# Paged attention in split fp32: the fourth head of each quad joins the split, and two small steps change engine

## The chip, the cores and the metric

One core of a Trainium2 chip runs the whole kernel. The metric is the device time in microseconds of one execution; the median of three runs is given. The engines are TensorE (PE in the profile, its weight loads PEld), VectorE (DVE), ScalarE (ACT), GpSimd (POOL) and SyncE (SP), which issues most of the DMAs.

## What is computed

32 sequences of 32 tokens, width 512. Layer one is attention over a paged cache: 32 query heads and 8 key heads of 128, 16 pages of 32 cached positions and the 32 new positions for each sequence.

```python
q = rope(rmsnorm(x @ Wq.T)); k = rope(rmsnorm(x @ Wk.T)); v = x @ Wv.T
k_all = concat([k_cache[table], k], axis=1)      # 512 cached + 32 new columns
v_all = concat([v_cache[table], v], axis=1)
scores = einsum('bqhd,bkhd->bhqk', q, k_all) * SCALE   # cached columns masked by length
probs = softmax(scores)                          # 4 query heads share a key head
o = einsum('bhqk,bkhd->bqhd', probs, v_all) @ Wo.T
```

A convolution along the sequence, an adapter layer and a gated feed-forward layer follow; the change doesn't touch them.

## The kernel before

The 32 sequences are done in two halves of HB = 16 (`Fori` over h). In a half come the projections with norm and rotation, then attention, then the output projection and the later layers. In attention every engine runs a written-out program of steps. A step is one key head g of one sequence b; 8 steps make a sequence, and `GU = 4` steps a quad. The four query heads that share a key head give 4 x 32 = 128 rows, so a step's scores are 128 rows by `LK` = 544 columns, 512 cached and 32 new.

Each engine works strictly through its own list, and counting semaphores order the engines among each other. For a head g:

- ScalarE (`upper_keys`, L781) rounds the keys of head g + 2 to fp32r, k_hi, when the scores of head g are done, since k_hi has two buffers. GpSimd (`lower_keys`, L605) forms the rest, keys minus k_hi. Queries are split once per quad: ScalarE writes q_hi (`upper_q`, L773) at g % 4 == 0, VectorE q_lo = q - q_hi (`lower_q`, L1512) at g % 4 == 1.
- TensorE (`scores`) adds q_hi k_hi, q_hi k_lo and q_lo k_hi, two matmuls each (288 and 256 columns), L1033 to L1044. That is so for three heads of a quad (`NS` = 3). The fourth head is scored in plain fp32 from q_now, a copy of the queries (L774), and the keys as loaded, L1021 and L1023, with no k_hi and no lowering.
- VectorE (L1553) scales by the row factor, adds the mask and takes the minimum in one pass into one of four probability buffers (`PRING`). ScalarE (L822) takes exp with the row sum, VectorE (L1563) the reciprocal of the sum.
- GpSimd (`scale_probs`) scales the 32 new columns into `prob_new` (L591) and the 512 cached ones in place (L593), two steps behind its lowering.
- TensorE transposes the cached part of head g - 2 (`turn_probs`, L1056) into one PSUM bank. VectorE copies that bank to SBUF (L1559), and TensorE multiplies by the values of head g - 3 (`values`, L1088). The next transposes wait until the copy has read the bank.
- Once per quad TensorE transposes the 128 new columns of four heads (`turn_new`, L1068, at g = 5 and g = 1). ScalarE copies four 32x128 quadrants of the result into the block diagonal of `spread` (`spread_new`, L800, at g % 4 == 1), which was cleared once. TensorE multiplies the new values by it (`values_new`, L1098, at g = 7 and g = 3), and ScalarE moves the finished quad out (`keep_o`, L807, at g % 4 == 0).

ScalarE's step, in its order: k_hi of head g + 2 (not where that is a fourth head), exp of g, at g % 4 == 0 q_hi and q_now and later `keep_o`, at g % 4 == 1 `spread_new`, at g = 3 the mask of the next sequence (L786, L787). VectorE's step: the reduction of g, the copy of transposed probabilities of g - 2, the reciprocal of g, at g % 4 == 1 q_lo. SyncE loads pages of keys and values two sequences ahead.

Of the kernel before, what the change touches and what calls it, by code (L numbers as in the profile page):

```python
# [13 lines left out]
ds = bass.ds  # L14
# [15 lines left out]
NS = GU - 1  # L30
NSB = UNITS * NS
# [29 lines left out]
               ("opr", 4), ("opi", 4), ("omr", 4), ("omi", 4)]  # L61
# [17 lines left out]
def constants():  # L79
# [13 lines left out]
    put("seqpos", (p % SEQ)[:, None])  # L93
    put("lmask", LORA_SCALING * (p[:, None] // RANK == np.arange(GRP * SEQ)[None, :] // SEQ))
# [11 lines left out]
def build(nc, xT_d, w_d, amat_d, bmT_d, kpages_d, vpages_d, lA_d, lB_d, rows_d, vcT_d, bp_d, dls_d,  # L106
# [6 lines left out]
    with ExitStack() as ctx:  # L113
# [24 lines left out]

        q_hi = sb("q_hi", [P, 2, NS * D], F32R)
        q_lo = sb("q_lo", [P, 2, NS * D], F32R)  # L140
        q_now = sb("q_now", [P, 2, D])
# [199 lines left out]
        q_copied = sem("q_copied")  # L341
# [10 lines left out]
        spread_clear = sem("spread_clear")  # L352
# [207 lines left out]
        def _(pool):  # L560
# [10 lines left out]
            with pool.Fori(0, HALVES) as h:  # L571
# [11 lines left out]
                def scale_probs(b, g, early=False):  # L583

                    u, a = g // GU, g % GU
                    pool.wait_ge(rinv_ready, h * STEPS + b * HK + g + 1)
                    if a == 0 and not early:
                        pool.wait_ge(new_turned, h * QUADS + b * UNITS + u - 1)
                    pool.sem_inc(pool_past, 1)
                    main, new = prob(g % PRING)[:, 0:LC], prob(g % PRING)[:, LC:LK]  # L590
                    nc.gpsimd.tensor_scalar(prob_new[:, u, a * SEQ:(a + 1) * SEQ], new, rinv[:, g:g + 1], 1.0,  # L591
                                            ALU.mult, ALU.mult).then_inc(new_scaled, 1)
                    nc.gpsimd.tensor_scalar(main, main, rinv[:, g:g + 1], 1.0, ALU.mult, ALU.mult)\  # L593
                        .then_inc(p_ready, 1)

                def lower_keys(b, par, first, last=False):


                    for g in range(HK):
                        s = h * STEPS + b * HK + g  # L600
                        if g % GU < NS:
                            e = g // GU * NS + g % GU
                            pool.wait_ge(khi_ready, (h * HB + b) * NSB + e + 1)
                            pool.sem_inc(pool_past, 1)
                            nc.gpsimd.tensor_tensor(  # L605
                                kbuf_lo(par)[:, :, g, :], kbuf(par)[:, :, g, :],
                                k_hi[:, e % 2, :].rearrange("p (j t) -> p j t", t=PSIZE), ALU.subtract)\
                                .then_inc(klo_ready, 1)
                        if g >= 2:
                            scale_probs(b, g - 2, first)  # L610
                        elif not first:
                            scale_probs(b - 1, g - 2 + HK)
# [31 lines left out]
        def _(act):  # L644
# [18 lines left out]
            with act.Fori(0, HALVES) as h:  # L663
# [107 lines left out]
                def upper_q(u, at):  # L771

                    nc.scalar.activation(q_hi[:, u, :], qo[:, ds(at, NS * D)], ACT.Copy).then_inc(qhi_ready, 1)  # L773
                    nc.scalar.activation(q_now[:, u, :], qo[:, ds(at + NS * D, D)], ACT.Copy).then_inc(q_copied, 1)  # L774

                def upper_keys(b, par, g):
# [3 lines left out]
                    e = g // GU * NS + g % GU  # L780
                    nc.scalar.activation(k_hi[:, e % 2, :].rearrange("p (j t) -> p j t", t=PSIZE),  # L781
# [8 lines left out]
                def spread_new(b, u):  # L790

                    act.wait_ge(new_turned, h * QUADS + b * UNITS + u + 1)
                    if isinstance(b, int) and b == 0 and u == 0:
                        act.wait_ge(spread_clear, h + 1)
                    else:
                        act.wait_ge(o_done, h * QUADS + b * UNITS + u)
                    act.sem_inc(act_past, 1)
                    for a in range(GU):
                        rows = slice(a * SEQ, (a + 1) * SEQ)
                        nc.scalar.activation(spread[rows, a * P:(a + 1) * P], PS[rows, 2560:2688], ACT.Copy)\  # L800
                            .then_inc(spread_ready, 1)
# [8 lines left out]
                def step(b, par, g, first, last=False):  # L810
                    s = h * STEPS + b * HK + g
                    if (g + 2) % GU < NS and not (last and g + 2 >= HK):
# [15 lines left out]
                    if g % GU == 1 and not (first and g < GU):  # L828
                        spread_new(b if g > GU else b - 1, int(g < GU))
# [34 lines left out]
                spread_new(HB - 1, 1)  # L864
# [53 lines left out]
        def _(pe):  # L918
# [9 lines left out]
            with pe.Fori(0, HALVES) as h:  # L928
# [76 lines left out]
                def scores(b, par, g, first):  # L1005
# [4 lines left out]
                    raw = kbuf(par)  # L1010
# [7 lines left out]
                    if a == NS:  # L1018
                        pe.wait_ge(q_copied, h * (QUADS + 1) + b * UNITS + u + 1)
                        pe.wait_ge(k_in[par], h * (136 * HB) + (b - par) * 136 + 272)  # L1020
                        nc.tensor.matmul(PS[:, at:at + mid], q_now[:, u, :], raw[:, 0:SPLIT, g, :],  # L1021
                                         start=True, stop=True)
                        nc.tensor.matmul(PS[:, at + mid:at + LK], q_now[:, u, :], raw[:, SPLIT:NPP + 1, g, :],  # L1023
                                         start=True, stop=True).then_inc(s_ready, 1)
                        return
                    if a == 0:
                        pe.wait_ge(qlo_ready, h * (QUADS + 1) + b * UNITS + u + 1)
                    e = u * NS + a
                    pe.wait_ge(khi_ready, (h * HB + b) * NSB + e + 1)
                    hi, lo = k_hi[:, e % 2, :], kbuf_lo(par)  # L1030
# [710 lines left out]
```

## Time and profile before

| | |
|---|---|
| median of 3 runs | 1304.55 us (1303.5 to 1306.85) |
| profiled execution | 1306.34 us, its span 1304.4 us |
| TensorE matmuls busy | 1246.8 us, 96% of the span |
| VectorE, ScalarE, GpSimd busy | 812.0, 809.2, 759.2 us |
| mean granted TensorE clock | 0.988 of full speed |
| read from HBM | 203.33 MB |

The profile comes from one execution. A busy time counts every moment in which an instruction of the engine was open; matmuls are pipelined, so their busy time can include waiting that follows on a chain elsewhere. Durations of one instruction include its start-up, and neighbours on an engine overlap a little, so distances from start to start are the safer measure.

### The profile page before, as it was taken

What the parts mean: (1) busy time and instruction counts of PE and PEld (TensorE: products, weight loads), DVE (VectorE), ACT (ScalarE), POOL (GpSimd) and SP (SyncE); (2) the same over time, 40 slices, a digit from 0 to 9 for tenths busy, and PEclk for the clock granted to TensorE, in tenths of its full rate; (3) what the DMA queues carried; (4) which work ended last, traced back from release to release, by engine and by line L of the source; (5) the groups of instructions that cost most, each with busy time, mean ns of one, the idle gap of its engine ahead of it and who ended that gap; (6) DMA issues with size and microseconds to landing.
All of it is one profiled execution on the core that took longest, in us unless ns stands there. A gap on an engine that the chain in (4) does not pass through costs nothing.

```text
span 1304.4 us, 28634 instructions
## 1 busy us (share of the span) xinstructions
PE 1246.8 (96%) x7378; PEld 1040.6 (80%) x7378; DVE 812.0 (62%) x1725; ACT 809.2 (62%) x2258; POOL 759.2 (58%) x885
## 2 busy tenths in 40 slices
PE   7899988999999998998999999889999999999998
PEld 6678877889999895764777788778989999878856
DVE  5976655776767766862328766556767767655422
ACT  5566766788878874332326766667878878743320
POOL 4344457788888874533214434568888888744330
PEclk9999999999999998998999999999999999999999
DMA  7244379999999935304243432798999999433300
GB/s 246 97 130 130 98 198 250 225 237 236 236 227 232 239 78 180 137 1 146 81 142 115 134 124 98 199 247 212 234 243 225 232 233 232 106 110 134 97 33 33
DMA packets 148008, 214.82 MB, mean 165 GB/s; under 512 B 24980, under 2 KB 119510, under 8 KB 142166
## 3 DMA queue, kind: packets, MB, share of 16 engines
q1 hardware_dynamic: 130566, 204.86, 58.6%
q10 hardware_dynamic: 17328, 9.04, 2.4%
q8 instruction: 30, 0.49, 0.2%
q14 instruction: 52, 0.43, 0.1%
q0 software_dynamic: 32, 0.00, 0.0%
HBM read 203.33 MB, written 10.49 MB: 164 GB/s over the span
## 4 chain that ended last, share of the span: by engine, by line
PE 77%; DVE 6%; SPq 5%; issue 4%; DMA 4%; ACT 2%; ACTq 1%; POOL 0%; DVEq 0%; POOLq 0%
PE PS L1088 15%; PE PS L1056 8%; PE PS L956 4%; PE PS L950 4%; PE PS L952 4%; PE PS L1098 4%; PE PS L1153 3%; PE PS L1150 3%; PE PS L1144 3%; PE PS L1195 2%; SPq L475 2%; PE PS L936 2%; SPq L462 2%; PE PS L1021 2%; PE PS L1023 2%
## 5 line engine op out<-in xcount | busy, mean ns | idle before, releaser
L605 POOL TENSOR_TENSOR kv_parts<-kv,k_hi 128x544 fp32r<-128x544 f32 x192 | 258.7, 1348 | 56.8 <-ACT k_hi L781 53.2
L1088 PE MATMUL PS<-probT,kv 128*128 128x128 f32 x2048 | 272.7, 277 | 6.9 <-DMA kv<-in_vpages 6.9
L1088 PEld LDWEIGHTS PS<-probT,kv 128*128 128x128 f32 x2048 | 250.6, 193 | 7.9 <-DMA kv<-in_vpages 6.0
L565 POOL TENSOR_TENSOR ring_parts<-ring,kv_parts 128x512 fp32r<-128x512 f32 x96 | 128.1, 1338 | 217.7 <-ACT kv_parts L671 187.8
L1559 DVE COPY probT<-PS 128x512 f32<-128x512 f32 x256 | 175.5, 686 | 3.1 <-PE PS L1056 3.1
L822 ACT ACTIVATE ring<-ring,smin 128x544 f32<-128x544 f32 x192 | 143.8, 749 | 45.6 <-DVE smin L1553 41.7
L1553 DVE CUSTOM_DVE_ANT_0 ring<-PS,mask,rq 128x544 f32<-128x544 f32 x192 | 149.8, 780 | 22.2 <-PE PS L1044 13.9
L781 ACT ACTIVATE k_hi<-kv 128x544 fp32r<-128x544 f32 x192 | 125.9, 656 | 60.4 <-PE PS L1044 52.3
L627 POOL TENSOR_TENSOR ring_parts<-ring,kv_parts 128x512 fp32r<-128x512 f32 x64 | 89.2, 1398 | 104.2 <-ACT kv_parts L876 104.2
L593 POOL TENSOR_SCALAR ring<-ring,rinv 128x512 f32<-128x512 f32 x192 | 135.3, 704 | 0.0
L1056 PE MATMUL PS<-consts,ring 128*128 128x128 f32 x768 | 117.7, 276 | 6.8 <-DVE probT L1559 5.9
L1589 DVE TENSOR_TENSOR qo_parts<-qo,kv_parts 128x512 fp32r<-128x512 f32 x64 | 83.0, 1322 | 63.4 <-ACT kv_parts L878 62.4
L591 POOL TENSOR_SCALAR ring<-ring,rinv 128x32 f32<-128x32 f32 x192 | 77.0, 401 | 72.9 <-DVE rinv L1563 72.9
L1056 PEld LDWEIGHTS PS<-consts,ring 128*128 128x128 f32 x768 | 88.2, 141 | 28.2 <-issue 19.8
L950 PE MATMUL PS<-kv_parts 128*128 128x512 f32 x352 | 103.4, 414 | 6.0 <-DVE PS L1474 4.7
L1153 PE MATMUL PS<-qo_parts,kv_parts 128*128 128x512 f32 x256 | 104.4, 408 | 4.9 <-DVE qo_parts L1589 4.9
L1144 PE MATMUL PS<-kv_parts 128*128 128x512 f32 x256 | 102.9, 402 | 4.3 <-ACT kv_parts L878 4.3
L876 ACT ACTIVATE kv_parts<-ring 128x512 fp32r<-128x512 f32 x64 | 40.3, 630 | 104.6 <-PE PS L1144 104.4
L1150 PE MATMUL PS<-kv_parts,ring_parts 128*128 128x512 f32 x256 | 102.5, 400 | 0.8 <-POOL ring_parts L627 0.8
L1553 DVE CUSTOM_DVE_ANT_0 prob<-PS,mask,rq 128x544 f32<-128x544 f32 x64 | 50.2, 784 | 82.0 <-PE PS L1044 80.9
L1563 DVE RECIPROCAL rinv<-rsum 128x1 f32<-128x1 f32 x256 | 41.9, 164 | 90.7 <-ACT ring L822 68.7
L1470 DVE TENSOR_TENSOR kv<-PS,kv 128x512 f32<-128x512 f32 x80 | 55.1, 689 | 67.4 <-ACT prob L706 39.6
(223 smaller groups left out, 2855.2 us busy)
## 6 DMA issues: line engine op xcount, KB each, us to landing
kv<-in_kpages SPq DMA_DIRECT2D x512, 128.0 KB, 2.8
kv<-in_vpages SPq DMA_DIRECT2D x512, 128.0 KB
ring<-in_w SPq DMA_DIRECT2D x44, 1024.0 KB, 4.9
v_new<-kv ACTq DMA_DIRECT2D x16, 256.0 KB, 4.8
k_new<-kv ACTq DMA_DIRECT2D x16, 256.0 KB, 2.4
kv<-k_new SPq DMA_DIRECT2D x32, 128.0 KB, 2.6
kv<-v_new SPq DMA_DIRECT2D x32, 128.0 KB
kv<-in_xT SPq DMA_DIRECT2D x8, 256.0 KB, 5.6
```

Of the source, the lines that this page charges most:

```text
L565: nc.gpsimd.tensor_tensor(slot_lo(n % SLOTS)[:, c, :], slot(n % SLOTS)[:, c, :], block_hi[:, (n % 2) * KC + c, :], ALU.subtract)\
L593: nc.gpsimd.tensor_scalar(main, main, rinv[:, g:g + 1], 1.0, ALU.mult, ALU.mult)\
L605: nc.gpsimd.tensor_tensor(kbuf_lo(par)[:, :, g, :], kbuf(par)[:, :, g, :], k_hi[:, e % 2, :].rearrange("p (j t) -> p j t", t=PSIZE), ALU.s ...
L822: nc.scalar.activation(a, a, ACT.Exp, scale=-1.0, bias=smin[:, g:g + 1], accum_out=rsum[:, g:g + 1]).then_inc(exp_done, 1)
L950: nc.tensor.matmul(dst, x_hi[:, c, ms], hi[:, c, :], start=(c == 0), stop=False)
L1056: mm = nc.tensor.transpose(PS[:, 2048 + c * P:2048 + (c + 1) * P], prob(g % PRING)[:, c * P:(c + 1) * P], ident)
L1088: mm = nc.tensor.matmul(PS[:, at:at + D], vbuf(bpar)[:, c, gg * D:(gg + 1) * D], probT[:, g % 2, c * P:(c + 1) * P], start=(c == 0 and a = ...
L1144: mm = nc.tensor.matmul(bank(c), whi[:, a, cs], ohi[:, a, :], start=(head == 0), stop=False)
L1150: nc.tensor.matmul(bank(c), w[:, cs], ohi[:, a, :], start=False, stop=False)
L1153: mm = nc.tensor.matmul(bank(c), whi[:, a, cs], o, start=False, stop=(head == HQ - 1))
L1553: V.tensor_tensor_reduce(prob(g % PRING)[:, 0:LK], PS[:, at:at + LK], mask[:, par, :], rq[:, par, g:g + 1], 3.0e38, ALU.add, ALU.min, smin ...
L1559: V.tensor_copy(probT[:, g % 2, :], bank(4)).then_inc(pt_main, 1)
```

## The change

All four heads of a quad are scored from the split parts. q_hi and q_lo get four heads of columns, q_now and its semaphore go, and k_hi and the lowering are done for every head. The 32 new columns are scaled by ScalarE (`scale_new`, one head behind its exp) instead of GpSimd. The block diagonal is written by VectorE in one product of the transposed columns, broadcast four times, with a constant 128x4 pattern (`quad`, 1 where row / 32 equals the column), broadcast along each block of 128; it stands behind q_lo at g % 4 == 1. ScalarE's four copies and the clearing of `spread` go.

```diff
...
-               ("opr", 4), ("opi", 4), ("omr", 4), ("omi", 4)]
+               ("quad", GU), ("opr", 4), ("opi", 4), ("omr", 4), ("omi", 4)]
...
+    put("quad", p[:, None] // SEQ == np.arange(GU)[None, :])
...
-        q_hi = sb("q_hi", [P, 2, NS * D], F32R)
-        q_lo = sb("q_lo", [P, 2, NS * D], F32R)
-        q_now = sb("q_now", [P, 2, D])
+        q_hi = sb("q_hi", [P, 2, GU * D], F32R)
+        q_lo = sb("q_lo", [P, 2, GU * D], F32R)
...
-    def scale_probs(b, g, early=False):
-        u, a = g // GU, g % GU
+    def scale_probs(b, g):
...
-        if a == 0 and not early:
-            pool.wait_ge(new_turned, h * QUADS + b * UNITS + u - 1)
...
-        main, new = prob(g % PRING)[:, 0:LC], prob(g % PRING)[:, LC:LK]
-        nc.gpsimd.tensor_scalar(prob_new[:, u, a * SEQ:(a + 1) * SEQ], new, rinv[:, g:g + 1], 1.0,
-                                ALU.mult, ALU.mult).then_inc(new_scaled, 1)
+        main = prob(g % PRING)[:, 0:LC]
...
         for g in range(HK):
-            s = h * STEPS + b * HK + g
-            if g % GU < NS:
-                e = g // GU * NS + g % GU
-                pool.wait_ge(khi_ready, (h * HB + b) * NSB + e + 1)
-                pool.sem_inc(pool_past, 1)
-                nc.gpsimd.tensor_tensor(
-                    kbuf_lo(par)[:, :, g, :], kbuf(par)[:, :, g, :],
-                    k_hi[:, e % 2, :].rearrange("p (j t) -> p j t", t=PSIZE), ALU.subtract)\
-                    .then_inc(klo_ready, 1)
+            pool.wait_ge(khi_ready, h * STEPS + b * HK + g + 1)
+            pool.sem_inc(pool_past, 1)
+            nc.gpsimd.tensor_tensor(
+                kbuf_lo(par)[:, :, g, :], kbuf(par)[:, :, g, :],
+                k_hi[:, g % 2, :].rearrange("p (j t) -> p j t", t=PSIZE), ALU.subtract)\
+                .then_inc(klo_ready, 1)
             if g >= 2:
-                scale_probs(b, g - 2, first)
+                scale_probs(b, g - 2)
             elif not first:
                 scale_probs(b - 1, g - 2 + HK)
...
     def upper_q(u, at):
-        nc.scalar.activation(q_hi[:, u, :], qo[:, ds(at, NS * D)], ACT.Copy).then_inc(qhi_ready, 1)
-        nc.scalar.activation(q_now[:, u, :], qo[:, ds(at + NS * D, D)], ACT.Copy).then_inc(q_copied, 1)
+        nc.scalar.activation(q_hi[:, u, :], qo[:, ds(at, GU * D)], ACT.Copy).then_inc(qhi_ready, 1)
     def upper_keys(b, par, g):
...
-        e = g // GU * NS + g % GU
-        nc.scalar.activation(k_hi[:, e % 2, :].rearrange("p (j t) -> p j t", t=PSIZE),
+        nc.scalar.activation(k_hi[:, g % 2, :].rearrange("p (j t) -> p j t", t=PSIZE),
...
-    def spread_new(b, u):
-        act.wait_ge(new_turned, h * QUADS + b * UNITS + u + 1)
-        if isinstance(b, int) and b == 0 and u == 0:
-            act.wait_ge(spread_clear, h + 1)
-        else:
-            act.wait_ge(o_done, h * QUADS + b * UNITS + u)
+    def scale_new(b, g):
+        u, a = g // GU, g % GU
+        act.wait_ge(rinv_ready, h * STEPS + b * HK + g + 1)
+        if a == 0 and not (isinstance(b, int) and b == 0):
+            act.wait_ge(new_turned, h * QUADS + b * UNITS + u - 1)
...
-        for a in range(GU):
-            rows = slice(a * SEQ, (a + 1) * SEQ)
-            nc.scalar.activation(spread[rows, a * P:(a + 1) * P], PS[rows, 2560:2688], ACT.Copy)\
-                .then_inc(spread_ready, 1)
+        nc.scalar.activation(prob_new[:, u, a * SEQ:(a + 1) * SEQ], prob(g % PRING)[:, LC:LK], ACT.Copy,
+                             scale=rinv[:, g:g + 1]).then_inc(new_scaled, 1)
...
-        if (g + 2) % GU < NS and not (last and g + 2 >= HK):
+        if not (last and g + 2 >= HK):
...
             upper_q(u, nb * (HQ * SEQ) + u * GU * D)
-        if g % GU == 1 and not (first and g < GU):
-            spread_new(b if g > GU else b - 1, int(g < GU))
+        if g:
+            scale_new(b, g - 1)
+        elif not first:
+            scale_new(b - 1, HK - 1)
...
-    spread_new(HB - 1, 1)
+    scale_new(HB - 1, HK - 1)
...
-        raw = kbuf(par)
...
-        if a == NS:
-            pe.wait_ge(q_copied, h * (QUADS + 1) + b * UNITS + u + 1)
-            pe.wait_ge(k_in[par], h * (136 * HB) + (b - par) * 136 + 272)
-            nc.tensor.matmul(PS[:, at:at + mid], q_now[:, u, :], raw[:, 0:SPLIT, g, :],
-                             start=True, stop=True)
-            nc.tensor.matmul(PS[:, at + mid:at + LK], q_now[:, u, :], raw[:, SPLIT:NPP + 1, g, :],
-                             start=True, stop=True).then_inc(s_ready, 1)
-            return
         if a == 0:
...
-        e = u * NS + a
-        pe.wait_ge(khi_ready, (h * HB + b) * NSB + e + 1)
-        hi, lo = k_hi[:, e % 2, :], kbuf_lo(par)
+        pe.wait_ge(khi_ready, s + 1)
+        hi, lo = k_hi[:, g % 2, :], kbuf_lo(par)
...
-        pe.wait_ge(klo_ready, (h * HB + b) * NSB + e + 1)
+        pe.wait_ge(klo_ready, s + 1)
...
-            pe.wait_ge(spread_ready, GU * (h * QUADS + b * UNITS + u))
+            pe.wait_ge(spread_ready, h * QUADS + b * UNITS + u)
         nc.tensor.transpose(PS[:, 2560:2688], prob_new[:, u, :], ident).then_inc(new_turned, 1)
...
-            pe.wait_ge(spread_clear, h + 1)
...
-        pe.wait_ge(spread_ready, GU * (h * QUADS + b * UNITS + u + 1))
+        pe.wait_ge(spread_ready, h * QUADS + b * UNITS + u + 1)
...
+    def spread_new(b, u):
+        dve.wait_ge(new_turned, h * QUADS + b * UNITS + u + 1)
+        if not (isinstance(b, int) and b == 0 and u == 0):
+            dve.wait_ge(o_done, h * QUADS + b * UNITS + u)
+        dve.sem_inc(dve_past, 1)
+        V.tensor_tensor(spread.rearrange("p (a x) -> p a x", a=GU),
+                        PS[:, 2560:2688].unsqueeze(1).to_broadcast([P, GU, P]),
+                        con("quad").unsqueeze(2).to_broadcast([P, GU, P]), ALU.mult)\
+            .then_inc(spread_ready, 1)
     def step(b, par, g, first):
...
-                lower_q(u, ds(nb * (HQ * SEQ) + u * GU * D, NS * D))
+                lower_q(u, ds(nb * (HQ * SEQ) + u * GU * D, GU * D))
+                if not (first and g < GU):
+                    spread_new(b if g > GU else b - 1, int(g < GU))
     for g in range(HK):
...
-            V.memset(spread, 0.0).then_inc(spread_clear, 1)
     for g in range(HK):
...
+    spread_new(HB - 1, 1)
...
```

## Rows read from the trace of the kernel before

**Rows 1.** Windows: length, busy us (and count) by engine, granted clock, DMA share, GB/s.
```profile
198.00:202.00 4.00, 1.55 (x13) 1.29 (x12) 1.73 (x5) 2.44 (x7) 4.00 (x6) 1.00 0.97 276
...
260.00:360.00 100.00, 100.00 (x759) 90.49 (x758) 70.45 (x178) 81.54 (x198) 85.16 (x115) 1.00 0.97 237
```

**Rows 2.** Timeline, first reduction of a quad: quads 1, 7 and 32, first half.
```profile
170.34 0.79 DVE L1553 CUSTOM_DVE_ANT_0 prob<-PS,mask,rq 128x544 f32<-128x544 f32 x1 [3.10 <-PE PS L1044]
...
236.79 0.78 DVE L1553 CUSTOM_DVE_ANT_0 prob<-PS,mask,rq 128x544 f32<-128x544 f32 x1 [1.13 <-PE PS L1044]
...
476.95 0.78 DVE L1553 CUSTOM_DVE_ANT_0 prob<-PS,mask,rq 128x544 f32<-128x544 f32 x1 [1.05 <-PE PS L1044]
```

**Rows 3.** Chain of waits in time order: start, us, engine and line.
```profile
367.11 0.49 PE PS L1021 x2
367.60 0.43 PE PS L1023 x2
368.03 0.51 PE PS L1056 x4
...
370.29 0.13 PE PS L1033
...
371.06 0.44 PE PS L1056 x4
```

**Rows 4.** Timeline of one quad, 361.7 to 371.4: start, us, engine, line, idle before.
```profile
361.72 0.78 DVE L1553 CUSTOM_DVE_ANT_0 prob<-PS,mask,rq 128x544 f32<-128x544 f32 x1 [1.07 <-PE PS L1044]
...
362.55 0.75 ACT L822 ACTIVATE prob<-prob,smin 128x544 f32<-128x544 f32 x1 [0.36 <-DVE smin L1553]
...
363.30 0.51 ACT L773 ACTIVATE q_hi<-qo 128x384 fp32r x1
...
364.03 0.60 ACT L807 ACTIVATE qo<-PS 128x512 f32 x1
...
364.63 0.75 ACT L822 ACTIVATE ring<-ring,smin 128x544 f32<-128x544 f32 x1
...
365.51 0.16 DVE L1563 RECIPROCAL rinv<-rsum 128x1 f32<-128x1 f32 x1 [0.30 <-ACT ring L822]
...
365.89 0.57 DVE L1512 TENSOR_TENSOR q_lo<-qo,q_hi 128x384 fp32r<-128x384 f32 x1 [0.22 <-issue]
...
366.38 0.77 DVE L1553 CUSTOM_DVE_ANT_0 ring<-PS,mask,rq 128x544 f32<-128x544 f32 x1
...
366.54 0.66 ACT L781 ACTIVATE k_hi<-kv 128x544 fp32r<-128x544 f32 x1
...
367.08 0.68 DVE L1559 COPY probT<-PS 128x512 f32<-128x512 f32 x1
...
367.38 1.34 POOL L605 TENSOR_TENSOR kv_parts<-kv,k_hi 128x544 fp32r<-128x544 f32 x1 [0.18 <-ACT k_hi L781]
...
367.88 0.42 PEld L1056 LDWEIGHTS PS<-consts,ring 128*128 128x128 f32 x4 [0.26 <-issue]
...
371.35 0.78 DVE L1553 CUSTOM_DVE_ANT_0 prob<-PS,mask,rq 128x544 f32<-128x544 f32 x1 [1.14 <-PE PS L1044]
```

**Rows 5.** Groups by line and shape: count, busy us and mean ns, idle before.
```profile
L1470 DVE TENSOR_TENSOR kv<-PS,kv 128x512 f32<-128x512 f32 x80 | 55.1, 689 | 67.4 <-ACT prob L706 39.6 <-ACT probT L706 27.8
...
L787 ACT ACTIVATE mask<-consts,lens_b 128x512 f32<-128x512 f32 x32 | 22.7, 709 | 0.0
```

**Rows 6.** The same groups between 360 and 372 us.
```profile
L593 POOL TENSOR_SCALAR ring<-ring,rinv 128x512 f32<-128x512 f32 x5 | 3.5, 695 | 0.0
...
L786 ACT ACTIVATE rq<-rowscale 128x8 f32 x1 | 0.2, 192 | 0.0
```

**Rows 7.** Timeline of VectorE and GpSimd, output projection, 563 to 565 us.
```profile
563.23 1.29 POOL L627 TENSOR_TENSOR ring_parts<-ring,kv_parts 128x512 fp32r<-128x512 f32 x1 [1.50 <-ACT kv_parts L876]
...
563.39 1.15 DVE L1398 TENSOR_TENSOR kv<-consts,kv 128x4 f32<-128x4 f32 x1
```

More of the change, by code:

```diff
@@ L29 @@
 UNITS = HK // GU
-NS = GU - 1
-NSB = UNITS * NS
 SLOTS = 4
@@ L340, in build @@
         qhi_ready = sem("qhi_ready")
-        q_copied = sem("q_copied")
         qlo_ready = sem("qlo_ready")
@@ L351, in build @@
         new_turned = sem("new_turned")
-        spread_clear = sem("spread_clear")
         spread_ready = sem("spread_ready")
@@ L1525, in norm_rows @@
                     dve.wait_ge(qhi_ready, h * (QUADS + 1) + 1)
-                    lower_q(0, slice(0, NS * D))
+                    lower_q(0, slice(0, GU * D))
                     dve.wait_ge(row_ready, 16 * (h + 1))
```

## The prediction

> **What bounds the kernel now.** I read the windows first, then TensorE's chain of waits, then the timeline of one group of four heads, because only the last can say what a change in the order of work is worth. The two attention loops are the stage that is edited: 2 halves, each 16 sequences of 8 key heads, so 64 groups of four heads ("quads"). The window shows TensorE busy for all of its 100 us at the granted clock 1.00, with GpSimd busy for 85, ScalarE for 82 and VectorE for 70 [rows 1]. From that alone one would call TensorE the bound and every other engine free. The distance between the first scores of consecutive quads is (476.95 - 236.79) / 25 = 9.61 us in the steady part [rows 2].
>
> The chain of waits shows what TensorE does with it [rows 3]. A head scored in fp32 takes 0.49 + 0.43 = 0.92 us, a head scored from the split parts takes 371.06 - 370.29 = 0.77 us. The four transposes behind the fp32 head take 0.51 us, those behind a split head 0.44. So the fp32 head is 0.15 us dearer, and 0.07 us of something else sits behind it.
>
> The timeline names that something [rows 4]. VectorE's copy of transposed probabilities (L1559) begins at 367.08 and lasts 0.68, thus ends at 367.76. TensorE's next weight load, for the next transposes, begins 0.12 us later at 367.88, with an idle of 0.26 us in front. The PSUM bank that the transposes write has to be copied out first. TensorE therefore waits once per quad on VectorE, briefly, and the busy share (a pipelined matmul counts as busy) hides it. Followed backwards from that copy, with t = 0 at the start of the quad's first reduction (361.72), the chain is: exp of head 4 on ScalarE at 0.83; q_hi at 1.58; keep_o at 2.31; exp of head 5 at 2.91; reciprocal of head 5 on VectorE at 3.79; q_lo at 4.17; the reduction of head 6 (L1553) at 4.66; the copy for head 4 at 5.36, its end at 6.04; and from there 371.35 - 367.76 = 3.59 us of transposes, values, new values and scores until the next quad's first reduction. 6.04 + 3.59 = 9.63 us. (Heads are counted as in the loop, g = 4 to 7 for this quad; g = 0 to 3 goes the same way.) There is no slack in this chain: each step of it starts when the one before ends, apart from hand-over times. Whatever the change puts into it is paid in every quad.
>
> **The change, part by part.**
>
> *TensorE.* The fourth head of each quad goes from 0.92 to 0.77 us and its transposes from 0.51 to 0.44: 0.22 us less, so TensorE alone could do a quad in 9.63 - 0.22 = 9.41 us. This is worth something only if VectorE's copy comes earlier by as much. It does not, as follows.
>
> *ScalarE at g = 4.* q_hi grows from 384 to 512 columns and q_now goes. Together these two took 364.03 - 363.30 = 0.73 us. q_hi of 512 columns should occupy 0.52 (a 128x512 copy lasts 0.60 [rows 4], and neighbours overlap by about 0.09). Behind it now comes scale_new of head 3, 32 columns with a per-partition scale. A 128x8 copy lasts 0.19, and a 128x512 operation with a per-partition bias 0.71 where the plain one lasts 0.60 [rows 4 to 6]: 0.19 + 0.02 + 0.11 less the overlap of 0.09 is 0.22 us. Bounds: nothing, if it slips into the overlap, and 0.32 without any overlap. Sum 0.74 for 0.73: keep_o still starts at 2.31. TensorE's transpose of the new columns waits for that scale_new, which ends at about 1.58 + 0.52 + 0.31 = 2.4, plus 0.1 of hand-over. If TensorE gets there earlier it waits, by an estimate some tenths. It then still reaches the transposes of g = 7, now at 6.16 (367.88), well before the 7.83 worked out below: up to 1.6 us of such a wait would vanish in the longer one.
>
> *ScalarE at g = 5.* Head 7 now is split too, so its k_hi stands before the exp of head 5, which had no such copy in front before. It waits for nothing (the scores of head 5 are long ready): 366.54 to 367.20 in the rows of head 8, +0.66 us. The exp of head 5 moves from 2.91 to 3.57; its mask and minimum are ready by 2.9, so nothing else hides this. Behind it in ScalarE's queue are scale_new of head 4, k_hi of head 8 and the exp of head 6. The four quadrant copies that leave ScalarE stood behind the exp of head 5, off the chain, so their going saves nothing.
>
> *VectorE at g = 5.* The reciprocal moves to 3.57 + 0.88 = 4.45 and q_lo becomes ready at 4.83. But GpSimd, which had no keys to lower here, now runs the lowering of head 7: it starts 0.84 after its k_hi (366.54 to 367.38), at 2.91 + 0.84 = 3.75, and lasts 1.34, to 5.09. A VectorE operation with two SBUF inputs does not run beside a GpSimd one: a product of 128x4 that needs 0.16 or so (as the reciprocal) took 1.15 us and ended at 564.54, when a GpSimd subtraction of 563.23 + 1.29 = 564.52 did [rows 7]. q_lo has two SBUF inputs, so it starts at 5.09: +0.26. Bounds: 0, if it is not held; +0.97, if GpSimd's next operation (the scaling of the probabilities, 0.70 us [rows 6]) is let in first. q_lo itself has 512 columns for 384: 0.49 / 384 x 128 is 0.16, less the fixed part 0.13 us. The new product follows, 128x512 with one PSUM and one SBUF input: the nearest row lasts 0.69 [rows 5] while GpSimd was working, so it is not held; neighbours overlap by 0.07, +0.62 us. Both its waits (the transposed columns, the last use of the buffer) are met by then. Its bounds are 0.62 and, if both broadcasts and a fresh fetch cost, 0.95. Queued behind it are the reduction of head 6 and the copy that TensorE waits for.
>
> *Sum for a quad.* 0.01 + 0.66 + 0.26 + 0.13 + 0.62 = 1.68, say 1.67 us: the copy ends at 7.71 instead of 6.04, and the transposes' load starts at 7.83. What follows the copy (3.59 us) contains no fp32 work and stays; its lower bound, should those transposes run without their present hitch, is 3.5. New period 11.3 us for 9.63.
>
> *What else fits.* GpSimd: four lowerings of 1.34 and four scalings of 0.70 are 8.2 us of 11.3; the small scalings that leave it had cover. ScalarE some 8 us. Neither decides. The keys of head 7 are lowered by 5.1, before TensorE, held by the transposes, can use all of them. The wider constants, the removed memset and the end of each half cost nothing: they lie beside TensorE's work, and the last spread takes 0.7 us on VectorE where ScalarE's four copies took more.
>
> *How many quads.* From the seventh quad on, 26 per half (25 intervals and the last quad's own), 52 in all: 52 x 1.67 = 87 us. The first six of a half take 236.79 - 170.34 = 66.5 us in the first half, 8.8 above the steady pace, and similar in the second, because pages are late. A slower quad hides those waits: 6 x 11.3 = 67.8, that is 1.3 us more than now if all overlaps and 10 if nothing does. I take 3 per half, 6. Together +93 us. The profiled execution lasted 1306.34 us with a span of 1304.4, 1.8 above the median of 1304.55; 1306.3 + 93 = 1399.3, and on the median's footing 1397.5 us.
>
> *A rule on the lock.* The Trainium skill, "SBUF — State Buffer", section "SBUF: two separate sides", says that the port pair shared by VectorE and GpSimd is an exclusive lock which whichever starts first keeps for the whole instruction. Rows 7 agree. By the rule q_lo must wait for the lowering, as summed; without it the sum would be 52 x 0.26 = 14 us less. The page does not say who comes first at the hand-over, so it also carries rival B.
>
> **The rivals.**
>
> A (forecast, 0.64): the chain as above, 1397.5 us. On its own, with the small bounds, 1380 to 1412.
>
> B (0.12): at 5.09 GpSimd's scaling takes the ports ahead of the waiting q_lo. Another 0.70 per quad, 52 x 0.70 = 36: 1434 us. For it: GpSimd's next operation is ready. Against: VectorE has been waiting longer.
>
> C (0.13): the exp of head 5 does not move, since what precedes it slips elsewhere, or q_lo is not held and the overlaps are kinder: 1.67 - 0.66 = 1.01 per quad, 52 x 1.01 + 6 = 59: 1363 us. Against: in the rows ScalarE goes from keep_o to that exp with no gap.
>
> D (0.06, other side): TensorE sets the pace and the insertions are absorbed; 9.41 for 9.63 gives 52 x 0.22 = 11 us less, 1293 us. It decides only if the copy has 1.7 us of slack before TensorE needs it. The rows show 0.12 us, the hand-over itself. For it speaks only the busy share.
>
> E (0.03): TensorE, now idle 1.6 to 1.9 us per quad, is granted the lower of its two clock levels (1.2 for 2.4 GHz) in places and its instructions in the chain take twice as long there; the stretch behind the copy, 3.59 us, is mostly its own, and over half the quads that is 26 x 3.59 = 93 more, 1490 us. Against: a stretch in which it was busy for 1.55 of 4 us had 1.00 granted all the same [rows 1].
>
> F (0.02): gain and cost cancel, 1304 us.
>
> **From this to the numbers.** A change within 0.3% (4 us) cannot be told from none here. Faster 0.06 (D), same 0.02 (F), slower 0.92 (A, B, C, E). The range runs from C's side, 1358, to B's, 1438; outside lie D, E, F and the ends of B and C.
>
> **What the new profile would show.** Quads 11.3 us apart; TensorE's busy share in the steady windows near 0.85, its main wait at the transposes of L1056 at g = 7 and 3, released by VectorE's copy; a k_hi between keep_o and the exp of head 5; q_lo longer than 0.7 us by its hold; the product at 0.69. The forecast is wrong if VectorE or ScalarE idle between those pieces, if the product costs much more than 0.69, or if quads come at 9.4.

## The result and the profile after

The changed kernel takes 1375.66 us (median of 4 runs, 1374.76 to 1377.74) against 1305.7 us for the kernel before in the same runs: a ratio of 1.0539, 95% interval 1.0515 to 1.0562, 70 us slower. The forecast was 1397.5 us in a range of 1358 to 1438. The profiled execution lasted 1377.74 us with a span of 1375.9, 71.5 us above the span before.

The busy times of the engines over the whole span, and the steady window that answers to [rows 1]:

```profile
PE 1251.8 (91%) x7506; PEld 1047.2 (76%) x7506; DVE 873.8 (64%) x1787; ACT 812.8 (59%) x2256; POOL 781.0 (57%) x693
```

```profile
260.00:360.00 100.00, 88.98 (x686) 80.62 (x685) 69.27 (x163) 71.72 (x176) 77.64 (x74) 1.00 0.82 204
```

TensorE is still the busiest engine. In the steady part all of them are less busy than before, TensorE at 89% for 100, VectorE at 69, ScalarE at 72, GpSimd at 78, and the granted clock is still 1.00. Every engine waits more, and no other engine has filled up: in a window, a chain across engines looks like this. The reductions that open a quad, quads 1, 7 and 32 of the first half (timeline, for [rows 2]):

```profile
169.96 0.78 DVE L1538 CUSTOM_DVE_ANT_0 prob<-PS,mask,rq 128x544 f32<-128x544 f32 x1 [2.97 <-PE PS L1019]
...
239.64 0.78 DVE L1538 CUSTOM_DVE_ANT_0 prob<-PS,mask,rq 128x544 f32<-128x544 f32 x1 [1.11 <-PE PS L1019]
...
513.50 0.78 DVE L1538 CUSTOM_DVE_ANT_0 prob<-PS,mask,rq 128x544 f32<-128x544 f32 x1 [1.07 <-PE PS L1019]
```

(513.50 - 239.64) / 25 = 10.95 us for 9.61 before. The first six quads take 69.7 us for 66.5.

One quad in the timeline answers to [rows 4]. L805 is the exp, L761 q_hi, L783 scale_new, L790 keep_o, L767 k_hi, L1548 the reciprocal, L1486 q_lo, L1520 the product, L1538 the reduction, L1544 the copy, L593 GpSimd's lowering, L584 its scaling and L1031 the transposes:

```profile
371.09 0.79 DVE L1538 CUSTOM_DVE_ANT_0 prob<-PS,mask,rq 128x544 f32<-128x544 f32 x1 [1.12 <-PE PS L1019]
...
371.92 0.75 ACT L805 ACTIVATE prob<-prob,smin 128x544 f32<-128x544 f32 x1 [0.42 <-DVE smin L1538]
...
372.67 0.61 ACT L761 ACTIVATE q_hi<-qo 128x512 fp32r x1
...
373.19 0.30 ACT L783 ACTIVATE ring<-ring,rinv 128x32 f32<-128x32 f32 x1
373.40 0.57 ACT L790 ACTIVATE qo<-PS 128x512 f32 x1
...
373.88 0.64 ACT L767 ACTIVATE k_hi<-kv 128x544 fp32r<-128x544 f32 x1
...
374.43 0.74 ACT L805 ACTIVATE ring<-ring,smin 128x544 f32<-128x544 f32 x1
...
374.71 1.35 POOL L593 TENSOR_TENSOR kv_parts<-kv,k_hi 128x544 fp32r<-128x544 f32 x1 [0.85 <-ACT k_hi L767]
...
375.29 0.16 DVE L1548 RECIPROCAL rinv<-rsum 128x1 f32<-128x1 f32 x1 [0.71 <-ACT ring L805]
...
375.70 0.91 DVE L1486 TENSOR_TENSOR q_lo<-qo,q_hi 128x512 fp32r<-128x512 f32 x1 [0.24 <-issue]
...
376.03 1.13 POOL L584 TENSOR_SCALAR ring<-ring,rinv 128x512 f32<-128x512 f32 x1
376.52 0.68 DVE L1520 TENSOR_TENSOR kv<-PS,consts 128x512 f32<-128x512 f32 x1
...
377.12 0.77 DVE L1538 CUSTOM_DVE_ANT_0 ring<-PS,mask,rq 128x544 f32<-128x544 f32 x1
...
377.82 0.68 DVE L1544 COPY probT<-PS 128x512 f32<-128x512 f32 x1
...
378.62 0.42 PEld L1031 LDWEIGHTS PS<-consts,ring 128*128 128x128 f32 x4 [1.21 <-issue]
...
382.03 0.78 DVE L1538 CUSTOM_DVE_ANT_0 prob<-PS,mask,rq 128x544 f32<-128x544 f32 x1 [1.08 <-PE PS L1019]
```

Over the whole execution the page counts it up, in the group of the transposes (the last two figures are the idle time in front of them and what ended it):

```profile
L1031 PE MATMUL PS<-consts,ring 128*128 128x128 f32 x768 | 118.4, 277 | 64.3 <-DVE probT L1544 64.2
```

Before, the matmuls of this line waited 5.9 us for that copy. The forecast's chain is there with each piece in its place, and at its end TensorE's weight load for the transposes, 0.12 us behind the copy's end (377.82 + 0.68 = 378.50) after 1.21 us of idle time, where [rows 4] had 0.26.

### The profile page after: what moved, and what is told of

Same layout as the page of the kernel before. It is cut to its first block, busy times and chain, and to the rows that moved or that the text cites. A ratio compares the mean times of both kernels' runs of the same rounds, so it can differ in the third digit from the quotient of the medians.

```text
span 1375.9 us, 28722 instructions
## 1 busy us (share of the span) xinstructions
PE 1251.8 (91%) x7506; PEld 1047.2 (76%) x7506; DVE 873.8 (64%) x1787; ACT 812.8 (59%) x2256; POOL 781.0 (57%) x693
## 4 chain that ended last, share of the span: by engine, by line
PE 52%; DVE 16%; issue 13%; ACT 11%; DMA 2%; SPq 2%; ACTq 2%; DVEq 1%; POOL 0%; POOLq 0%
PE PS L1063 5%; PE PS L935 4%; PE PS L941 4%; PE PS L937 4%; PE PS L1072 4%; PE PS L1031 3%; PE PS L1127 3%; DVE ring L1538 3%; PE PS L1118 3%; PE PS L1124 3%; DVE kv L1520 3%; ACT ring L805 3%; DVE probT L1544 3%; ACT q_hi L761 2%; PE PS L1169 2%
## 5 line engine op out<-in xcount | busy, mean ns | idle before, releaser
L593 POOL TENSOR_TENSOR kv_parts<-kv,k_hi 128x544 fp32r<-128x544 f32 x256 | 343.8, 1343 | 136.6 <-ACT k_hi L767 136.6
L1063 PEld LDWEIGHTS PS<-probT,kv 128*128 128x128 f32 x2048 | 254.6, 195 | 0.6 <-DMA kv<-in_vpages 0.4
L805 ACT ACTIVATE ring<-ring,smin 128x544 f32<-128x544 f32 x192 | 143.0, 745 | 128.5 <-DVE smin L1538 128.5
L767 ACT ACTIVATE k_hi<-kv 128x544 fp32r<-128x544 f32 x256 | 166.1, 650 | 51.3 <-PE PS L1019 39.0
L584 POOL TENSOR_SCALAR ring<-ring,rinv 128x512 f32<-128x512 f32 x192 | 161.0, 839 | 49.5 <-DVE rinv L1548 48.5
L1544 DVE COPY probT<-PS 128x512 f32<-128x512 f32 x256 | 175.3, 685 | 3.1 <-PE PS L1031 3.1
L1031 PE MATMUL PS<-consts,ring 128*128 128x128 f32 x768 | 118.4, 277 | 64.3 <-DVE probT L1544 64.2
L1538 DVE CUSTOM_DVE_ANT_0 ring<-PS,mask,rq 128x544 f32<-128x544 f32 x192 | 149.6, 779 | 22.5 <-PE PS L1019 14.0
L1031 PEld LDWEIGHTS PS<-consts,ring 128*128 128x128 f32 x768 | 88.5, 142 | 78.4 <-issue 74.6
L1008 PE MATMUL PS<-k_hi,q_hi 128*128 128x288 f32 x256 | 116.0, 453 | 2.2 <-ACT k_hi L767 2.2
L1548 DVE RECIPROCAL rinv<-rsum 128x1 f32<-128x1 f32 x256 | 42.0, 164 | 113.5 <-ACT ring L805 91.6
L1538 DVE CUSTOM_DVE_ANT_0 prob<-PS,mask,rq 128x544 f32<-128x544 f32 x64 | 50.2, 784 | 74.4 <-PE PS L1019 73.3
```

The costliest lines, as they stand in the source:

```text
L593: nc.gpsimd.tensor_tensor(kbuf_lo(par)[:, :, g, :], kbuf(par)[:, :, g, :], k_hi[:, g % 2, :].rearrange("p (j t) -> p j t", t=PSIZE), ALU.s ...
L767: nc.scalar.activation(k_hi[:, g % 2, :].rearrange("p (j t) -> p j t", t=PSIZE), kbuf(par)[:, :, g, :], ACT.Copy).then_inc(khi_ready, 1)
L805: nc.scalar.activation(a, a, ACT.Exp, scale=-1.0, bias=smin[:, g:g + 1], accum_out=rsum[:, g:g + 1]).then_inc(exp_done, 1)
L1031: mm = nc.tensor.transpose(PS[:, 2048 + c * P:2048 + (c + 1) * P], prob(g % PRING)[:, c * P:(c + 1) * P], ident)
L1063: mm = nc.tensor.matmul(PS[:, at:at + D], vbuf(bpar)[:, c, gg * D:(gg + 1) * D], probT[:, g % 2, c * P:(c + 1) * P], start=(c == 0 and a = ...
L1538: V.tensor_tensor_reduce(prob(g % PRING)[:, 0:LK], PS[:, at:at + LK], mask[:, par, :], rq[:, par, g:g + 1], 3.0e38, ALU.add, ALU.min, smin ...
```

## The experiments

Each is timed against the kernel before on the same chip (its medians there lay between 1304.97 and 1306.06 us). "Pace" is the distance between quads from the seventh to the last of the first half, read from the timeline as in [rows 2]. An operation "occupies" the distance from its start to the start of the next one on its engine. The chain theory says that only what stands between the exp of the quad's first head and the copy that TensorE waits for is paid. Its rivals say that an engine's load is what costs (GpSimd has 33% more lowering), or TensorE's wait for the scaled new columns.

**The two halves of the change alone.** First the kernel before with only the two steps that change engine; the fourth head stays in fp32:

```diff
 # scores, q_hi, q_lo, q_now, k_hi, lowering: as before (NS = 3)
+ ScalarE: scale_new(b, g - 1) behind the exp;  VectorE: spread_new behind q_lo
- GpSimd: scaling of the 32 new columns;  ScalarE: four quadrant copies; memset
```

> The kernel before with only the two steps that change engine (new columns scaled on ScalarE, block diagonal by one product on VectorE); the fourth head stays in fp32. Chain theory: scale_new puts 0.21 us ahead of keep_o and the exp of head 5, the product 0.60 us ahead of the reduction of head 6, so a quad takes 0.8 us more than 9.61: about 1348 us. Rival, GpSimd's extra lowering is what costs: GpSimd has less to do here than before, so 1305 us. Rival, TensorE's wait for scale_new is what costs (0.22 us per quad): 1319 us.

Measured: 1335.29 us, ratio 1.0236 (1.0201 to 1.0271), pace 10.17 us. The load and wait rivals' 1305 and 1319 are both off; the chain theory is right in kind and 13 us too high, since it counted scale_new as paid. The timeline of this kernel (L767 is q_hi, L798 keep_o, L1556 and L813 the minimum of the reduction and the exp) shows why not:

```profile
367.61 0.51 ACT L767 ACTIVATE q_hi<-qo 128x384 fp32r x1
...
368.44 0.57 ACT L798 ACTIVATE qo<-PS 128x512 f32 x1
...
368.85 0.08 DVE L1556 DVE_READ_ACCUMULATOR2_ANT smin<- 128x1 f32 x1
...
368.96 0.75 ACT L813 ACTIVATE ring<-ring,smin 128x544 f32<-128x544 f32 x1
```

The exp of head 5 starts 2.92 us into the quad (its first reduction is at 366.04), as before (2.91). From q_hi to keep_o it is 0.83 us with scale_new in between, for 0.73 before, and keep_o occupies 0.52 for 0.60: ScalarE's queue had some 0.2 us of small waits in it, the last of them for the minimum, which ends at 368.93. Then the kernel before with only the fourth head split:

```diff
-        if (g + 2) % GU < NS and not (last and g + 2 >= HK):   # ScalarE: k_hi for every head
+        if not (last and g + 2 >= HK):
 # likewise the lowering, q_hi and q_lo with GU * D columns, scores without the fp32 branch
 # scaling of new columns stays on GpSimd, the block diagonal on ScalarE
```

> The kernel before with only the fourth head split too; the scaling stays on GpSimd and the block diagonal on ScalarE. Chain theory: q_now's 0.2 us net leaves ScalarE, the k_hi of head 7 adds 0.43 ahead of the exp of head 5, q_lo with 512 columns and its hold adds 0.33: about +0.55 us per quad, 1335 us; the two parts' costs add up to the whole change (10.95 - 9.61 = 1.34 us). Rival, GpSimd's work sets the pace: it has 4 x 1.34 + 4 x 0.7 + 4 x 0.3 = 9.4 us per quad here and in addition the hand-overs, more than in the changed kernel, so not faster than that one: 1375 us or more.

Measured: 1336.72 us, ratio 1.026 (1.0214 to 1.0306), pace 10.27 us; the chain theory's 1335 us is met within 2. This kernel has the most GpSimd work of all and is 39 us faster than the changed one, so GpSimd's load is not what costs. The halves cost 0.56 and 0.66 us per quad, 1.22 together, against 1.34 for the whole: nearly additive. Of the 0.12 us that are left, 0.08 can be seen: with a k_hi behind keep_o the exp no longer waits for its minimum, so scale_new is paid there in part. The exp of head 5 starts 3.34 us into the quad in the changed kernel (374.43 - 371.09) and 3.26 us in this one (370.73 - 367.47).

**Each suspected piece taken out of the chain by moving it.** The product to the next step:

```diff
                             lower_q(u, ...)                       # at g % GU == 1
-                            spread_new(...)
+                        if g % GU == 2 and not (first and g < GU):
+                            spread_new(...)
```

> The changed kernel with the product moved on VectorE from behind q_lo (g % 4 == 1) to behind the reciprocal of g % 4 == 2, where TensorE's new-value product gives the next transposes 0.86 us more. Same work on every engine. Chain theory: 0.60 us less per quad, about 1343 us. Rival, the busy time of VectorE or GpSimd counts and not the place: 1375 us.

Measured: 1343.47 us, ratio 1.0303 (1.0264 to 1.0341), pace 10.42 us, 0.53 less than the changed kernel. The exp ahead of k_hi:

```diff
 # ScalarE's step at g % GU == 1
-  k_hi(g + 2); exp(g); scale_new(g - 1)
+  exp(g); k_hi(g + 2); scale_new(g - 1)
```

> The changed kernel with ScalarE's k_hi of the next head moved behind the exp at g % 4 == 1. Same work on every engine. Chain theory: the exp of head 5 comes 0.43 us earlier, and q_lo is then ahead of GpSimd's lowering of head 7 and not held, 0.2 us: about 0.65 us less per quad, 1341 us, unless TensorE now waits for the lowering of head 7. Rival, GpSimd's lowering of the fourth head sets the pace: it starts later here, so slower than 1375 us.

Measured: 1341.33 us, ratio 1.027 (1.0235 to 1.0306), pace 10.31 us, 0.64 less. Both kernels do the same work as the changed one, and each gives back 32 to 34 us by order alone. In the second one q_lo comes ahead of GpSimd's lowering of head 7 and is not held (0.69 us), and the lowering is (1.60 us for 1.34). Its weight loads show the next wait in line already (L1019 is the lowered keys' matmul, L1036 the transposes):

```profile
368.67 0.19 PEld L1019 LDWEIGHTS PS<-kv_parts,q_hi 128*128 128x128 f32 x1 [0.35 <-POOL kv_parts L593]
369.43 0.42 PEld L1036 LDWEIGHTS PS<-consts,ring 128*128 128x128 f32 x4 [0.21 <-POOL ring L584]
```

Both are released by GpSimd.

**The lock by itself.**

```diff
+                        n = 1 if g % GU == GU - 1 else NPP + 1     # pages lowered
-                            kbuf_lo(par)[:, :, g, :], kbuf(par)[:, :, g, :], ...
+                            kbuf_lo(par)[:, 0:n, g, :], kbuf(par)[:, 0:n, g, :], ...
 # TensorE takes hi in place of lo for the fourth head
```

> The changed kernel, but GpSimd lowers only the first of 17 pages of the fourth head of each quad, and TensorE takes the upper part in place of the lower one there, with the same number of matmuls: left out is the lower part of a quarter of the keys. Chain theory: q_lo is no longer held by that lowering, 0.22 us less per quad, and nothing else: about 1363 us. Rival, GpSimd's load sets the pace: 1.1 to 1.2 us less per quad, about 1310 us.

Measured: 1363.16 us, ratio 1.0459 (1.0436 to 1.0481), pace 10.71 us. Taking 1.1 us of GpSimd's work per quad away gives 0.24 us, about the 0.22 that q_lo is shorter. The timeline of this kernel (L594 the slim lowering, L1491 q_lo, L584 the scaling):

```profile
368.55 0.25 POOL L594 TENSOR_TENSOR kv_parts<-kv,k_hi 128x32 fp32r<-128x32 f32 x1 [0.85 <-ACT k_hi L768]
...
369.51 1.20 POOL L584 TENSOR_SCALAR ring<-ring,rinv 128x512 f32<-128x512 f32 x1 [0.70 <-DVE rinv L1553]
369.54 0.69 DVE L1491 TENSOR_TENSOR q_lo<-qo,q_hi 128x512 fp32r<-128x512 f32 x1 [0.24 <-issue]
```

q_lo now takes 0.69 us for 0.91, and GpSimd's scaling stretches from 0.69 to 1.20 beside it.

**TensorE's wait for the new columns.**

```diff
 # ScalarE's step at g % GU == 0, behind the exp
-  upper_q; scale_new(g - 1); keep_o
+  scale_new(g - 1); upper_q; keep_o
```

> The changed kernel with scale_new ahead of q_hi on ScalarE at g % 4 == 0. TensorE's wait for the scaled new columns (0.22 us per quad in the trace) goes; ScalarE's sum up to the exp of head 5 stays. Chain theory: that wait lies ahead of the longer one for VectorE's copy, so no change: 1375 us. Rival, each wait of TensorE is paid: 64 x 0.22 = 14 us less, 1361 us.

Measured: 1376.88 us, ratio 1.0563 (1.0541 to 1.0585), pace 10.95 us. The wait is gone from the trace, and the time stays. The transpose of the new columns (L1043) in the changed kernel, and then here:

```profile
373.55 0.33 PE L1043 MATMUL PS<-consts,ring 128*128 128x128 f32 x1 [0.22 <-ACT ring L783]
```

```profile
368.60 0.27 PE L1043 MATMUL PS<-consts,ring 128*128 128x128 f32 x1
```

What TensorE no longer waits there, it waits at the transposes of g = 7: the idle time in front of that weight load is 1.67 us for 1.21.

```profile
374.06 0.42 PEld L1031 LDWEIGHTS PS<-consts,ring 128*128 128x128 f32 x4 [1.67 <-issue]
```

**Both pieces into VectorE's idle time.** VectorE waits for the exp in front of each reciprocal; the pieces fit there.

```diff
 # VectorE's step behind the copy
+  if g % GU == 1: lower_q(u, ...)
+  if g % GU == 2: spread_new(...)
   reciprocal(g)
-  if g % GU == 1: lower_q(u, ...); spread_new(...)
 # ScalarE: scale_new ahead of upper_q, as above
```

> The changed kernel with VectorE's two extra pieces put into its idle time ahead of the reciprocal: q_lo at g % 4 == 1, the product at g % 4 == 2; scale_new ahead of q_hi. Same work. Chain theory: q_lo and the product leave the chain; q_lo now starts ahead of GpSimd's lowering of head 7 and holds that up instead, so that the scaled probabilities of head 5 come 0.1 to 0.2 us late: 9.41 + 0.15 = 9.5 to 9.6 us per quad, 1298 to 1305 us. Rival, the engines' loads with four lowerings are what costs: above 1340 us.

Measured: 1295.27 us, ratio 0.9931 (0.9914 to 0.9949), pace 9.47 us: faster than both kernels, by 9.7 us (6 runs against 17) and by 80 us, and 3 us below the lower end of what was expected. Most quads take 9.39 to 9.46 us. In the timeline (L1555 is the reciprocal here) q_lo comes before GpSimd's lowering and holds it (1.68 us for 1.34). q_lo ends before the reciprocal. The product, one step later, ends some 0.2 us after the exp's row sum is there (347.45) and delays the reciprocal by that, but GpSimd, which uses the reciprocal, is busy with its lowering until 348.57:

```profile
344.63 0.74 ACT L805 ACTIVATE ring<-ring,smin 128x544 f32<-128x544 f32 x1
344.70 0.68 DVE L1486 TENSOR_TENSOR q_lo<-qo,q_hi 128x512 fp32r<-128x512 f32 x1
344.90 1.68 POOL L593 TENSOR_TENSOR kv_parts<-kv,k_hi 128x544 fp32r<-128x544 f32 x1 [0.84 <-ACT k_hi L767]
...
345.49 0.16 DVE L1555 RECIPROCAL rinv<-rsum 128x1 f32<-128x1 f32 x1
...
347.09 0.68 DVE L1520 TENSOR_TENSOR kv<-PS,consts 128x512 f32<-128x512 f32 x1
347.23 1.34 POOL L593 TENSOR_TENSOR kv_parts<-kv,k_hi 128x544 fp32r<-128x544 f32 x1
...
347.69 0.15 DVE L1555 RECIPROCAL rinv<-rsum 128x1 f32<-128x1 f32 x1
```

**The same for the kernel before**, which has only q_lo to move:

```diff
 # VectorE's step at g % GU == 1, behind the copy
+  lower_q(u, ...)
   reciprocal(g)
-  lower_q(u, ...)
```

> The kernel before with q_lo ahead of the reciprocal at g % 4 == 1, in VectorE's idle time. Chain theory: the chain of the kernel before had no slack only because q_lo stood in it; without it TensorE sets the pace, 9.63 - 0.07 to 0.1 us per quad: 4 to 6 us less, about 1301 us. Rival, TensorE set the pace before already: no change, 1305.7 us.

Measured: 1301.42 us (12 runs against 17), ratio 0.9983 (0.9965 to 1.0), pace 9.59 us. It is 3.5 us less, at the edge of what can be told from nothing. Most quads of the first half take 9.5 us, but some take 9.7 to 9.9. In the one of 9.9 the profile has TensorE waiting for a page of values that the faster quads have caught up with (L1088):

```profile
321.90 1.13 PE L1088 MATMUL PS<-probT,kv 128*128 128x128 f32 x8 [0.24 <-DMA kv<-in_vpages]
```

In one of 9.73 us the load of the same line comes 0.3 us late too, but the profile names no cause for it. The DMA share from 260 to 460 us is 0.99, for 0.95 before. That the loads take back a part of what the gap frees is shown for one quad and likely for the others.

The second half has no such quads from the eighth on, and shows what TensorE can do. From the seventh reduction to the last its pace is 9.51 us, for 9.61 in the kernel before:

```profile
890.01 0.78 DVE L1553 CUSTOM_DVE_ANT_0 prob<-PS,mask,rq 128x544 f32<-128x544 f32 x1 [1.15 <-PE PS L1044]
...
1127.78 0.78 DVE L1553 CUSTOM_DVE_ANT_0 prob<-PS,mask,rq 128x544 f32<-128x544 f32 x1 [1.05 <-PE PS L1044]
```

The last 20 quads of that half take 9.55 and 9.43 us in turn, 9.49 on average, with the fourth head still in fp32. TensorE's weight loads for that head, its transposes and the values behind them:

```profile
1056.98 0.30 PEld L1021 LDWEIGHTS PS<-kv,q_now 128*128 128x128 f32 x2
1057.33 0.43 PEld L1023 LDWEIGHTS PS<-kv,q_now 128*128 128x128 f32 x2
1057.79 0.57 PEld L1056 LDWEIGHTS PS<-consts,ring 128*128 128x128 f32 x4
1058.33 0.97 PEld L1088 LDWEIGHTS PS<-probT,kv 128*128 128x128 f32 x8
```

From L1021 to L1088 it is 1.35 us without a wait. In the kernel before, the same stretch of the quad of [rows 4] takes 1.44 us, with 0.26 us of idle time in it.

**The other order of the pieces.** Exp ahead of k_hi, product at g % GU == 1 and q_lo at g % GU == 2, both ahead of the reciprocal:

```diff
 # VectorE, behind the copy
-  if g % GU == 1: lower_q(u, ...)
-  if g % GU == 2: spread_new(...)
+  if g % GU == 1: spread_new(...)
+  if g % GU == 2: lower_q(u, ...)
 # ScalarE at g % GU == 1
-  k_hi(g + 2); exp(g)
+  exp(g); k_hi(g + 2)
```

> As the version with both pieces in VectorE's idle time, but with the exp of g % 4 == 1 ahead of k_hi, the product at g % 4 == 1 and q_lo at g % 4 == 2. ScalarE's and VectorE's chain is then short, but the lowering of head 7 starts 0.8 us later, at about 4.4 us into the quad instead of 3.6, and on GpSimd the scaling of head 5's probabilities stands behind it until about 6.5, where TensorE wants them at 6.2. Chain theory: GpSimd's queue becomes the chain, 9.41 + 0.4 us per quad: about 1315 us. Rival, only ScalarE and VectorE matter: 9.41 us per quad, 1293 us.

Measured: 1345.09 us, ratio 1.0291 (1.0259 to 1.0323), pace 10.42 us. The rival is out by 52 us, and my own figure by 30. The timeline and TensorE's loads of one quad that starts at 339.90:

```profile
344.39 1.34 POOL L593 TENSOR_TENSOR kv_parts<-kv,k_hi 128x544 fp32r<-128x544 f32 x1 [1.73 <-ACT k_hi L767]
...
345.48 0.81 DVE L1491 TENSOR_TENSOR q_lo<-qo,q_hi 128x512 fp32r<-128x512 f32 x1
...
345.72 1.12 POOL L584 TENSOR_SCALAR ring<-ring,rinv 128x512 f32<-128x512 f32 x1
```

```profile
345.78 0.19 PEld L1019 LDWEIGHTS PS<-kv_parts,q_hi 128*128 128x128 f32 x1 [0.49 <-POOL kv_parts L593]
346.89 0.42 PEld L1036 LDWEIGHTS PS<-consts,ring 128*128 128x128 f32 x4 [0.56 <-POOL ring L584]
```

The lowering starts at 4.49 us, as forecast. But TensorE waits for it directly too (0.49 us), which I had not counted, and q_lo goes ahead of the scaling, which is 0.43 us longer for it. Together these are 0.49 + 0.56 = 1.05 us; with the 9.43 us that quads take on average in the version without these waits (last 20 quads of its second half) that is 10.48, near the 10.42 measured. This version differs from the faster one in two things at once, ScalarE's order and the order of the two pieces; no run separates them.

## Why the prediction was right, and where it was off

*What bounds the kernel.* Right: the copy of transposed probabilities was without slack, hidden under a TensorE busy for 100% of the window. Shown from both sides: moving pieces out of the chain with the same work gives 32 to 34 us each, while 1.1 us of GpSimd's work and TensorE's wait for the new columns, taken away, give 12.5 us (the hold's part) and nothing.

*TensorE's saving of 0.22 us per quad, worth nothing here.* Right that it is worth nothing here, but the size is wrong. The fp32 head and its transposes were read where TensorE waits for the copy, so a part of that wait was counted as work. Without the wait they take 1.35 us up to the values, in the kernel before with q_lo moved, and a split head 1.20 (1056.09 - 1054.89 in the same trace): 0.15 us. The version with both pieces in the gaps has quads of 9.46 and 9.41 us in turn where that kernel has 9.55 and 9.43 (last 20 quads of the second half), 0.06 us less on average. Of the 0.18 us per quad by which it beats the kernel before, 0.12 come from taking q_lo out of the chain and only 0.06 go with the split of the fourth head and the rest of the change.

*ScalarE at g = 4, sum unchanged.* Right: keep_o starts 2.31 us into the quad, as before. scale_new occupies 0.21 for the 0.22 summed.

*k_hi ahead of the exp of head 5, +0.66.* Right in place, too large: 374.43 - 371.09 = 3.34 for 2.91, +0.43. I took the duration of a k_hi, but in ScalarE's queue it occupies 0.55. And the 0.60 us between keep_o and the exp before was not all keep_o: with k_hi behind it keep_o occupies 0.48, and the rest was the exp waiting for its minimum. That minimum ends at 364.60 in the kernel before, 0.03 us ahead of the exp (364.63):

```profile
364.52 0.08 DVE L1553 DVE_READ_ACCUMULATOR2_ANT smin<- 128x1 f32 x1
```

The prediction says that nothing else hides this, since the minimum is ready by 2.9; it was ready at 2.88, and the exp began at 2.91 because of it.

*q_lo.* Held, as forecast, and longer by its columns: from its start to the product's 0.82 us for 0.49, +0.33 for the 0.39 summed. VectorE, waiting, was let in ahead of GpSimd's scaling, which took 1.13 us for 0.69, so rival B is out. The slim lowering gives the hold alone, 0.24 us.

*The product.* It occupies 0.60 for the 0.62 summed.

*The sum.* The terms as measured are 0.43, 0.33 and 0.60, less 0.05 at the hand-overs and in what follows the copy (3.53 for 3.59 us): 1.31 us in the quad shown, 1.34 on average, against 1.67. From the seventh quad to the last of both halves that makes 67 us. The first six quads add 3.2 us in the first half, where 3 was forecast, and nothing in the second (68.5 us, for 68.8 before), where 3 was forecast too. The rest of the program adds 1.4, and the profiled execution is 71.5 us longer. The sum was too high by 0.33 us per quad, 17 of the 22 us by which the forecast was too high: 12 of them are the ScalarE term (0.23 us per quad), the step that was off, and 5 the small excesses of q_lo, product and the stretch behind the copy.

*The rivals.* The time lies 4 us below the lower end of 1380 that A was given and 13 above C's 1363. A's mechanism is the one seen: the exp moved and q_lo was held. Of C, only the kinder overlaps came, and in part: the exp moved by 0.43 us of 0.66. So the forecast's path was right and its range held the time, but its own narrow bounds did not. D is out: the copy had no slack, and TensorE did not set the pace. E did not come up: the clock stayed at 1.00 with TensorE at 89%.

## What to carry to other kernels

When every engine is at 70 to 90% and one shows 100, look in the timeline for the instruction whose start follows another engine's end by one hand-over. Here, what was put between it and its predecessors was paid nearly in full, whatever the shares said: 1.31 us of 1.36. Put small pieces where their engine waits anyway, ahead of the instruction that it waits to issue, and check what a moved piece locks or delays on the next engine: of the two orders that look alike here one gains 10 us and the other loses 39. In this case a piece inserted in a busy queue cost its start-to-start distance, and less where what followed it had been waiting for something else. And read what an engine saves from a stretch in which it doesn't wait: the 0.22 us read beside a wait were 0.15 at most.

## What was not expected of the hardware

When GpSimd's lowering ended here, VectorE's q_lo, which had been waiting, was let in ahead of GpSimd's next operation: q_lo, issued at 375.70 during a lowering that ended at 376.06, was done at 376.61, and the scaling issued at 376.03 took 1.13 us. The Trainium skill, "SBUF — State Buffer", section "SBUF: two separate sides", has the lock kept for a whole instruction, with which this agrees; who comes next it leaves open. The same lock is seen from the other side in the version in the gaps, where a lowering issued 0.20 us behind q_lo takes 1.68 us for 1.34.

Whether q_lo was let in because it had waited longer, or because VectorE goes first when both want the ports, is not shown. With the slim lowering neither had been waiting: GpSimd's scaling starts at 369.51 and q_lo at 369.54 by the profile, and still the scaling takes 1.20 us and q_lo 0.69. No run has GpSimd waiting while VectorE brings a second operation with two SBUF inputs, which would tell the two apart.
